# Attention's output projection: four plain 32-bit matmuls in place of twelve rounded passes

## The reference, cut to what matters

```python
def _layer(x, wqkv, qs, ksc, wo, lg, lb, w1, b1, w2, b2):
    ...
    o = local_attention(q, k, v)               # 8 heads of 64
    o = o.transpose(0, 2, 1, 3).reshape(b, n, INNER)   # INNER = 512
    x = x + o @ wo                             # wo: 512 x 256
    ...                                        # gated FFN, w1 and w2
x = x + 0.5 * _L0_ffn_ref(_layernorm(x), ...)  # two layers
x = x + _L0_attn_ref(_layernorm(x), ...)       # linear attention
x = x + 0.5 * _L0_ffn_ref(_layernorm(x), ...)  # two layers
...                                            # ternary FFN, gated layer, ternary FFN
```

## Time and profile before

| | |
|---|---|
| median of 3 runs | 3195.17 us (3194.49 to 3196.07) |
| span of the profiled execution | 3193.4 us, 99022 instructions |
| TensorE busy | 3068.6 us (96%), 35586 matmul records |
| VectorE busy | 2350.6 us (74%) |
| ScalarE busy | 1729.0 us (54%) |
| GpSimd busy | 1622.9 us (51%) |
| DMA | 122.82 MB, mean 38 GB/s |

### The profile page before, as it was taken

The page is one execution under the profiler, slowest core; times in us unless marked ns, Lnnn a source line. Parts: engine busy times, 40 slices in busy tenths (PEclk is TensorE's granted clock), DMA queues, the critical chain, the costliest instruction groups (busy, mean ns, idle before and its releaser), DMA issues.

```text
span 3193.4 us, 99022 instructions
## 1 busy us (share of the span) xinstructions
PE 3068.6 (96%) x35586; PEld 2681.3 (84%) x35586; DVE 2350.6 (74%) x6543; ACT 1729.0 (54%) x4532; POOL 1622.9 (51%) x1839
## 2 busy tenths in 40 slices
PE   6999999999999999999899999989999899999889
PEld 5888878878887888998788878878888788888778
DVE  6888767677776787777777767767777688777766
ACT  4767642266767224665667672237767622454445
POOL 7777730177776224333777761037777444317610
PEclk9999999999999999999999999999999999999999
DMA  4211121021111101000211112102111200100001
GB/s 135 67 45 44 37 81 33 23 63 40 36 40 39 42 20 43 11 10 21 58 40 36 40 39 76 30 26 66 37 39 34 72 21 13 27 0 1 1 14 40
DMA packets 178774, 122.82 MB, mean 38 GB/s; under 512 B 27533, under 2 KB 175337, under 8 KB 178025
## 3 DMA queue, kind: packets, MB, share of 16 engines
q1 hardware_dynamic: 177432, 117.77, 13.8%
q10 hardware_dynamic: 1104, 1.90, 0.2%
HBM read 48.29 MB, written 20.98 MB: 22 GB/s over the span
## 4 chain that ended last, share of the span: by engine, by line
PE 87%; DVE 6%; issue 3%; POOL 1%; ACT 1%; DMA 1%; SPq 0%; DVEq 0%; POOLq 0%; ACTq 0%
PE bank L347 15%; PE bank L348 13%; PE bank L349 13%; PE bank L511 8%; PE bank L480 6%; PE bank L452 3%; PE bank L732 2%; PE bank L731 2%; PE bank L730 2%; PE bank L724 2%; PE bank L725 2%; PE bank L489 2%; PE bank L676 2%; PE bank L675 2%; PE bank L490 2%
## 5 line engine op out<-in xcount | busy, mean ns | idle before, releaser
L2652 POOL TENSOR_TENSOR prob<-prob,rsum 128x384 f32<-128x384 f32 x512 | 416.2, 834 | 155.8 <-DVE rsum L1861 155.8
L1209 ACT ACTIVATE prob<-prob,nmax 128x192 f32<-128x192 f32 x1024 | 455.8, 454 | 2.2 <-DVE nmax L1854 2.2
L1401 ACT ACTIVATE gate<-bank,bias 128x512 f32<-128x512 f32 x192 | 132.4, 690 | 512.0 <-PE bank L349 511.9
L2639 POOL TENSOR_TENSOR rn<-ss,mhalf 128x16 f32<-128x16 f32 x128 | 375.9, 2937 | 10.7
L1854 DVE CUSTOM_DVE_ANT_0 prob<-bank,masks,rn 128x192 f32<-128x192 f32 x768 | 275.1, 414 | 100.1 <-PE bank L480 99.3
L2646 POOL TENSOR_TENSOR qk<-rot_t 128x512 f32<-128x512 f32 x256 | 331.9, 1297 | 23.3 <-DVE ss L1828 21.3
L347 PE MATMUL bank<-wqkv_hi,hT_hi 128*128 128x512 f32 x768 | 329.5, 429 | 14.7 <-DVE rot_t L1816 6.1
L2620 POOL TENSOR_TENSOR rstd<-meanvar,eps 128x4 f32<-128x4 f32 x48 | 12.4, 259 | 620.4 <-DVE meanvar L1786 620.4
L348 PE MATMUL bank<-wqkv_lo,hT_hi 128*128 128x512 f32 x768 | 303.0, 395 | 0.0
L349 PE MATMUL bank<-wqkv_hi,hT_lo 128*128 128x512 f32 x768 | 302.8, 394 | 0.0
L347 PE MATMUL bank<-gT_hi,w_hi 128*128 128x512 f32 x704 | 277.2, 394 | 2.6 <-issue 2.6
(11 more groups left out here) (292 smaller groups left out, 9831.1 us busy)
## 6 DMA issues: line engine op xcount, KB each, us to landing
Vlo<-V SPq DMA_DIRECT2D x256, 64.0 KB, 2.0
Vhi<-V SPq DMA_DIRECT2D x256, 64.0 KB, 2.0
H<-Y SPq DMA_DIRECT2D x128, 64.0 KB, 1.8
H<-ya SPq DMA_DIRECT2D x128, 64.0 KB, 1.8
yb<-Y SPq DMA_DIRECT2D x128, 64.0 KB, 1.6
HB<-Y SPq DMA_DIRECT2D x32, 256.0 KB, 2.8
HB<-yb SPq DMA_DIRECT2D x32, 256.0 KB, 3.1
raw<-in_L_ffn_wqkv SPq DMA_DIRECT2D x4, 1536.0 KB, 8.3
```

Source lines behind the costliest of these rows:

```text
L1209: ins = e.activation(pb, pb, ACT.Exp, bias=nm[r][:, x:x + 1], scale=-1.0, accum_out=sums[r][:, x:x + 1])
L2639: e.tensor_tensor(rn[u][:, :], ss[:, :], mhalf[:, :], ALU.pow).then_inc(s_plRN, 1)
L2652: e.tensor_tensor(pair, pair, rs[:, 2 * gi:2 * gi + 2].unsqueeze(2).to_broadcast([P, 2, KW]), ALU.mult).then_inc(s_plPN[gi], 1)
```

## The change

`wo_hi` and `wo_lo` become one 32-bit tile, `wo_full`, and a tile of the same size that keeps the memory layout (`wo_rest`, unused). `OT_hi` and `OT_lo` become one tile, `OT`. ScalarE copies both whole. TensorE's `wo_` issues four plain 32-bit matmuls of 128x128 weights by 256 columns. VectorE's `ot_` and GpSimd's `wo_weights` are gone, with the semaphore `s_dvOT`; `pv_` and `wo_` wait for ScalarE's `s_acOT` in its place. After slot 1 TensorE waits for ScalarE's copy of the weights; the count of `s_prepB` is one lower.

```diff
-        wo_h, wo_l = sb("wo_hi", [P, KI, D], F32R), sb("wo_lo", [P, KI, D], F32R)
+        wo_full = sb("wo_full", [P, KI, D])
+        sb("wo_rest", [P, KI, D])
...
-        OTh, OTl = sb("OT_hi", [P, INNER], F32R), sb("OT_lo", [P, INNER], F32R)
+        OT = sb("OT", [P, INNER])
...
                 def pv_(T, u, hf):
...
-                    e.wait_ge(s_dvOT, G + OFF)
+                    e.wait_ge(s_acOT, G + OFF)
...
                 def wo_(T, u):
                     G = R0 + T
-                    e.wait_ge(s_dvOT, G + 1 + OFF)
+                    e.wait_ge(s_acOT, G + 1 + OFF)
                     bank_free(T, (y_read, -1), (y_read, -2), (y_read, -3))
                     for c in range(KI):
                         lt = slice(c * P, (c + 1) * P)
-                        i = three(bank[7][:, 0:D], OTh[:, lt], OTl[:, lt], wo_h[:, c, :], wo_l[:, c, :], c == 0, c == KI - 1)
+                        i = e.matmul(bank[7][:, 0:D], OT[:, lt], wo_full[:, c, :], start=c == 0, stop=c == KI - 1)
                     i.then_inc(s_peWO, 1)
...
-                    if u < 2:
-                        e.wait_ge(s_prepB, need['B'] + 4 + u + OFF)
+                    if u == 0:
+                        e.wait_ge(s_prepB, need['B'] + 4 + OFF)
+                    if u == 1:
+                        e.wait_ge(s_prepA, need['A'] + 4 + OFF)
...
-                e.activation(flat(wo_h[:, :, :]), raw2[:, 0:KI * D], ACT.Copy).then_inc(s_prepA, 1)
+                e.activation(flat(wo_full[:, :, :]), raw2[:, 0:KI * D], ACT.Copy).then_inc(s_prepA, 1)
...
-                    e.activation(OTh[:, :], bank[6][:, :], ACT.Copy).then_inc(s_acOT, 1)
+                    e.activation(OT[:, :], bank[6][:, :], ACT.Copy).then_inc(s_acOT, 1)
...
-                def ot_(T, u):
-                    G = R0 + T
-                    e.wait_ge(s_acOT, G + 1 + OFF)
-                    e.tensor_tensor(OTl[:, :], bank[6][:, :], OTh[:, :].bitcast(F32), ALU.subtract).then_inc(s_dvOT, 1)
...
-            def wo_weights():
-                e.wait_ge(s_prepA, need['A'] + 4 + OFF)
-                e.tensor_tensor(flat(wo_l[:, :, :]), raw2[:, 0:KI * D], flat(wo_h[:, :, :]).bitcast(F32), ALU.subtract).then_inc(s_prepB, 1)
```

More of the change, by code:

```diff
@@ L293, in build @@
         s_pePV, s_dvRS = ([sem(f"{x}{h}") for h in range(2)] for x in ("s_pePV", "s_dvRS"))
-        s_acOT, s_dvOT, s_peWO, s_dvY, s_plM0, s_dvST = sem("s_acOT"), sem("s_dvOT"), sem("s_peWO"), sem("s_dvY"), sem("s_plM0"), sem("s_dvST")
+        s_acOT, s_peWO, s_dvY, s_plM0, s_dvST = sem("s_acOT"), sem("s_peWO"), sem("s_dvY"), sem("s_plM0"), sem("s_dvST")
         s_dvAG, s_plRV, s_dvXN, s_peTR, s_acHI, s_dvLO = sem("s_dvAG"), sem("s_plRV"), sem("s_dvXN"), sem("s_peTR"), sem("s_acHI"), sem("s_dvLO")
@@ L314, in build @@
                       *s_acKT, *s_peS, *s_dvMX, *s_acEX, *s_plPN, *s_pePT, *s_acPT, *s_pePV, *s_dvRS,
-                      s_acOT, s_dvOT, s_peWO, s_dvY, s_plM0, s_dvST, s_dvAG, s_plRV, s_dvXN, s_peTR, s_acHI, s_dvLO,
+                      s_acOT, s_peWO, s_dvY, s_plM0, s_dvST, s_dvAG, s_plRV, s_dvXN, s_peTR, s_acHI, s_dvLO,
                       s_dvGH, s_peG, s_peA, s_acU, s_dvHD, s_xxHH, s_acHH, s_dvHL, s_peW2, s_dvYB, s_peHF, s_sHB, s_mdvY,
@@ L368, in prep_A @@
                 prep['V'] += 2
-                prep['B'] += 5
+                prep['B'] += 4
             def pass_A(run, ffn_first):
@@ L1906, in slot @@
                         qk_(T + 2, (u + 2) % U, 0)
-                    if inside(T - 2):
-                        ot_(T - 2, (u - 2) % U)
                     if inside(T):
@@ L2598, in prep_A @@
                     e.memset(V[U - 1][:, :], 0.0).then_inc(s_prepB, 1)
-                    wo_weights()
             def v_weights():
```

## The result

The changed kernel takes 3236.64 us (median of four runs, 3234.57 to 3239.62) against 3195.57 us for the kernel before beside it: 1.013 of its time, 95% interval 1.0116 to 1.0144. The profiled execution spans 3236.7 us, 43.3 more than before.

What follows compares the result with a forecast made beforehand. TensorE's own blocks were taken to bound the steady slots. 120 tiles x 0.359 = +43.1 us, less 4.3 us gained from removed subtraction and weight copies, gives +38.8 on the profiled span; forecast median 3234.0 us, range 3224 to 3249.

Steps and rivals of the forecast that it cites:

- the sign: Whole kernel: the change makes it slower by more than the 0.2% a measurement can tell, chance 0.94.
- the carrying term: TensorE's output projection block: 0.359 us longer per tile, paid by 120 tiles, +43.1 us.
- What bounds the kernel: Steady attention slots of 12.20 us: TensorE's own blocks set the time, with no waits on other engines between blocks.
- The rival that VectorE's queue sets the slot: Attention slots: the longer block fills a gap, only gains at the beginnings are left, 3191 us; chance 0.03.
- The record of 256 columns: TensorE's output projection: each plain matmul is two records of 0.2207 us, eight per block, 1.766 us.
- the high end: Upper bound for a plain 256-column record: a 512-column rounded matmul's 0.23 us, block 1.84 us, +0.435 per tile.
- The Trainium skill's four passes: Output projection block: 16 passes at the rounded 0.1173 us, 1.877 us, +0.470 per tile, 3247 us in all.
- open weight loads: Rival on TensorE's plain records: weight loads not hidden, 0.10 us more per record, +96 us, 3330 us; chance 0.03.
- single stream: Rival on TensorE's plain records: columns streamed only once, 0.117 us per record, 3135 us; chance 0.03.
- Covered tiles: Ends of attention passes: existing TensorE waits hide the longer block in two of 32 tiles per pass; 120 tiles pay.
- VectorE's subtraction: Removing it (0.681 us per tile) gains nothing in steady slots and 0.1 us at each attention pass's end.
- The weight copies: GpSimd's dropped weight subtraction at attention pass starts: gains 2.34 + 0.9 in the third, 0.5 first, 0.1 each others.

Runs made afterwards that it cites:

- e3_low_parts_gone: Changed kernel without VectorE's and GpSimd's subtractions, but with TensorE's twelve rounded passes as in the kernel before (low parts not computed rightly); 3197.25 us, ratio 1.0006.
- e4_two_halves: Changed kernel with each plain matmul of 256 columns cut into two of 128, 16 records per block; 3245.86 us (two runs).
- e1_block_only: Kernel before with only the output projection's block made four plain matmuls; both subtractions still run, their results unread; 3233.49 us, ratio 1.0118.
- run 0: Not a follow-up kernel: the first of four attention passes inside every execution, numbered from 0, each with 32 tiles; no time of its own as an experiment.
- e2_wait_kept: Changed kernel in which VectorE still waits for ScalarE's output copy where its subtraction stood, doing nothing there; 3231.21 us, repeated 3230.61 us.
- e5_recip_early: Kernel before with the last tile's two row-sum reciprocals moved to before and after the FFN statistics on VectorE; 3179.51 us, ratio 0.9954.
- e6: Changed kernel with the last tile's two row-sum reciprocals moved to before and after the FFN statistics on VectorE; 3219.94 us.

## Why the prediction was right, and where its steps were off

The forecast was 3234.0 us with a range of 3224 to 3249; the kernel takes 3236.6. Both the sign and the carrying term were right. Under the sum, three terms were off. That they partly cancel is luck: the slots came 4.0 us shorter than expected, the run ends 3.7 and the rest 4.9 longer.

**What bounds the kernel: right.** Slots grew by 0.33 us with the block, and in e3_low_parts_gone they stayed at 12.21 with all the work off VectorE. The rival that VectorE's queue sets the slot is out.

**The record of 256 columns: mis-sized by 2%.** It was put at 0.2207 us and measures 0.216, a hair under the low end of 0.217. (By its own two terms the figure is 0.2205, and the high end's +0.435 is +0.433; neither changes the forecast.) The term 120 x 0.359 = 43.1 becomes 120 x 0.328 = 39.4. e4_two_halves splits the error: a record of 128 columns measures 0.111 us, not 0.1125, and another 128 columns add 0.105, not 0.108. The larger part is the growth. It had been taken from 0.058 us for one column half in `pv_` as a smaller record of the same kind, but those alternate between two halves. The Trainium skill's four passes ("FP8 and Floating Point Precision", TensorE Precision Notes) fit in number if each of the two records of a matmul is two passes; no run shows the passes themselves. At the rounded pass's 0.1173 they gave 1.877 us; the eight records take 1.73, which is 0.108 for a pass.

**The open weight loads and the single stream: both out.** Records 0.216 us apart allow neither; e4_two_halves hid sixteen loads in a block of 1.88 us. The loads are drawn at 190 ns against 187 for the rounded ones.

**Covered tiles: right as reasoned, with a cover that the change itself took away elsewhere.** In e1_block_only, where nothing but the block changed, the wait at run 2's end went from 3.33 to 3.00 us, by what the block grew, and at run 0's end by more. In the changed kernel the waits at run 0's end did not shrink by 0.36; they became 3.67.

**VectorE's subtraction: the step that failed.** Its work was rightly costed at nothing in the slots. At the run ends I named the 0.62 us that ended with it and counted +0.1 us of gain in each run. I didn't look at the wait in front of it, 2.51 us for ScalarE's copy, nor at what was queued behind it. Removing the instruction removed the wait, let `w1_piece(1)` start at once, and that piece held up GpSimd's multiplications, for which TensorE waits. The Trainium skill has the rule ("SBUF — State Buffer", Who interferes with whom): a VectorE instruction with two SBUF inputs contends with a GpSimd instruction that reads SBUF, for a pair of ports that is locked by one of them at a time. The trace agrees. The first multiplication runs from 435.64 and takes 0.83 us; the piece, begun at 435.88, takes 1.94 instead of 1.49 us, to 437.82; the second multiplication, begun at 436.43, takes 2.07 instead of 0.82, to 438.50. So each was held up about until the one before it was over. The end pieces were to gain the 0.4 us and pay tile 30's block, 4 x 0.359: +1.0 us. They cost 4.7 (4.4 in the second profile), 0.1 and 0.2 of it in runs 0 and 1, 1.4 and 3.1 in runs 2 and 3. e2_wait_kept gives back 5.2 of it. The sum also had no term for the clock at the run ends, though the half clock there can have cost 5 to 12 us in the kernels with the reciprocals in their old place, by the table.

The wait for `gT` before the first FFN matmul is what was named as late next: it grew from 0.64 to 1.23 us.

**The weight copies: about right at run 2's start, and not seen in the sum.** Counted were 3.9 us at the runs' starts, 3.2 of them in run 2. Run 2's wait, 4.70, was to be 2.36 and is 1.91 + 0.71:

```profile
1557.60 0.30 PE L490 MATMUL bank<-misc,prob 128*128 128x128 f32 x1 [1.91 <-issue]
...
1558.83 0.48 PE L490 MATMUL bank<-misc,prob 128*128 128x128 f32 x1 [0.71 <-POOL prob L2643]
```

In e3_low_parts_gone the stretch that ends with run 2's first block is 3.1 us shorter than before: 2.05 is this wait, and the half clock can have cost 1.7 less. That answers to the 2.34 + 0.9 of the prediction. The 0.5 us ahead of run 0's first block did not come (+0.2). The other 1.4 of its 3.8 us lie between run 2's FFN and run 3's first block, where the kernel before was at the half clock for some microseconds and this one was not. e5_recip_early, which keeps every copy, is 1.4 us shorter there too, so this part is not the removals' doing.

In the changed kernel "rest" is nevertheless 1.0 and 0.0 over before. Three things took the gain. At run 2's start the clock gave nothing back (it can have cost 3.4 us in both its profiles, as before; 1.7 in e3_low_parts_gone). Ahead of run 3's first block it can have cost 1.7 more than before. And in the first FFN groups of runs 0 and 1 there is a wait that I had not foreseen, 1.32 and 1.28 us. (Against them stand 1.8 us less in all that follows run 3's first FFN matmul, which the change does not touch; I have no cause for these.) The wait in run 0:

```profile
463.96 1.09 PE L668 MATMUL bank<-misc,Xn 128*128 128x128 f32 x8 [1.32 <-DVE Xn L2040]
```

Its chain can be followed back. VectorE's statistics for these tokens wait for the load of `HB`, and SyncE issues that load late. First SyncE's timeline of before, whose first FFN matmul starts at 440.19, then SyncE's and VectorE's of the changed kernel, where it starts at 449.47:

```profile
442.13 0.67 SPq L3070 DMA_DIRECT2D HB<-Y  x1
```

```profile
453.18 0.68 SPq L3059 DMA_DIRECT2D HB<-Y  x1
...
456.99 1.41 DVE L1782 BATCH_NORM_STATS2 stats<-HB 128x6 f32<-128x256 f32 x4 [2.40 <-DMA HB<-yb]
```

The load is 3.71 us behind the first FFN matmul instead of 1.94, because the store of Y ahead of it (`yb<-Y`) took 3.5 us to land instead of 1.5. Why the store was slow is open. The wait is in runs 0 and 1 of every profile of the changed kernel, of e1, e2 and e6, and not there in before or e3_low_parts_gone (0.4 us at most), so it looks like the longer block's; but e4_two_halves, with the longest block, has it in run 2 and not in runs 0 and 1. In run 3 the kernel before has such a wait too (1.29 us). So it depends on more than the block's length, and no experiment was made on it.

**The sum.** From tile 0 to 29, 41.6 us were expected (116 x 0.359) and 37.6 came; from tile 29 to the FFN 1.0 and 4.7; in the rest -3.9 and +1.0. That is 38.8 and 43.3 us on the profiled executions. By the medians it is 41.1.

## What to carry to other kernels

Before you take an instruction out, read the wait in front of it and the instruction behind it: if the wait was an accident that kept two engines apart, the removal brings them together. Count a matmul's form by the start-to-start time of its records, on the engine that sets the slot; relieving engines that idle anyway pays for none of it. And when a comparison leads you to a wait of some microseconds, ask whose order makes it, and look at the clock behind it: moving two reciprocals of 0.17 us each gave 15.9 us here, a good part of it by the clock, while all the removed work together (e3_low_parts_gone) gave nothing.

## What the hardware showed that I had not expected

- VectorE's `w_lo` piece (both inputs in SBUF) and GpSimd's multiplication lengthen each other to 1.94 and 2.07 us, from 1.49 and 0.82.
- Plain 32-bit records on the full array start 0.216 us apart at 256 columns and 0.111 at 128, each with a weight load of its own; a rounded pass of 256 columns takes 0.1173. A plain matmul of 256 columns is thus 0.432 us against 0.352 for the three rounded passes.
- After a wait of 3.33 us TensorE ran at 1.2 GHz for about 6 us of work. With waits of 0.54 and 1.48 us in the same place the clock stayed at 2.4 GHz in run 0, and with 0.54 and 1.49 it fell in run 1. The clock after a wait can cost as much as the wait, and whether it falls differed between two runs with the same waits.
